# Local attention masks laid into two PSUM banks by ScalarE instead of TensorE, with three of ScalarE's tasks moved in its queue

## The chip, the cores and the metric

The kernel runs on one core of a Trainium2 chip. The metric is the device time of one launch in microseconds (us), the median of several runs. TensorE (PE in the profile) does the matrix products, VectorE (DVE) and ScalarE (ACT) the elementwise work, GpSimd (POOL) more of it, and SyncE's queue (SPq) issues the transfers.

## The reference

The input x is 8 x 256 x 128. After a layer norm xn, the output is x + A(xn) + F(xn). A is one causal attention (16 heads of 64, keys and values through a rank of 128). F is a stack of 6 layers, and nearly all the time goes there. Each layer is

```python
x = attn_layer(shift_tokens(x), Wqkv, q_scale, k_scale, Wo) + x
x = ffn_layer(shift_tokens(x), g, b, W1, b1, W2, b2) + x

# attn_layer: q, k are l2-normalised per head, scaled, rotated; then, in windows of 32 queries
# over 64 keys (the window before and its own):
mask = (it < jb) | (it > jb + w) | (jb == -1)
sim = einsum(q, keys) * 8;  sim = where(mask, -max, sim)
out = einsum(softmax(sim), values)
# ffn_layer: layer norm, a, gate = x @ W1 + b1; (a * gelu(gate)) @ W2 + b2
```

## The kernel before

The causal attention A and the input norm fill the first 335 us. After that a stream of 192 slots, `slot(s)` for s = 0 to 191, does the six layers: a slot is one group of 4 heads of one of the 8 batch elements of one layer (6 x 8 x 4 = 192). The order of each engine's work inside a slot is written out by hand, once per engine, and semaphores tie the engines together. Each slot overlaps stages of several groups. In slot s:

- **TensorE** turns the weights of group s-1 (`turn_windows`, L984: 4 transposes), then computes the scores of group s (`windows`: two bf16 products that put the mask into the two banks of `pair_bank`, L965, and 64 small products that add the scores, L974), the keys of group s+4 (L1005 to L1007), a part of the output projection (L926), the norms of group s+3 (L958), the values times weights of group s-1 (`weigh_windows`, L996), one step of the feed-forward part when there is one (gate product L1057, up product L1071, down product L1079), the queries (L1005 to L1007) and values (L1017 to L1019) of group s+4, and sometimes two products of a layer norm (L1093, L1101).
- **VectorE** takes the maximum of the scores and subtracts it (`shift_windows`, L1289, L1291), rotates the keys (L1310, L1311), sums the exponentials and multiplies by the reciprocal (`weigh_down`, L1296, L1298, L1301, which signals `weights_ready`), bounds the norms (L1390), and rotates the queries when their squares are done (again L1310, L1311). The residual of the feed-forward part (L1325) comes first in a slot with s mod 8 = 5.
- **ScalarE**, in this order: `values_out` (L561, values from PSUM to `v_sb`), `spread_out` (L630, two activations), the table load back to exp and ln in a slot after a GELU (L681), the deviations of a layer norm (L636, L639), the exponential of the scores in place in both banks (L686), ln and exp of the norms (L690, L693), squares of the keys (L621), the rotary tables at a layer change (L601 to L609), the squares of a layer norm (L650), its gain (`gained`, L644), `output_out` (L657, into `yt`), the gate copy (L715), GELU with its table load (L661, L663), the squares of the queries (L621), the GELU of the last third (L667).
- **GpSimd** adds the rotated halves (L431), normalises keys and queries (L424) and adds the squares (L451). At a layer change it also splits the next layer's weights (L412, L419).
- **SyncE's queue** moves the normalised keys and queries into `zqk` (L350, 8 transfers a slot) and the values into `v_late` (L356, L357).

The feed-forward part repeats every 8 slots (`mlp_slot(s, first)`: s mod 8 equals first mod 8, 24 times from `first` on). From slot 13 on the gate copies lie in slots with s mod 8 = 5, 6 and 7, the GELU in those with 0 (22 times inside the stream, slots 16 to 184), and the table load back to exp and ln in those with 1. A layer is 32 slots; there are 5 layer changes.

`turn_windows(n)` waits for `weights_ready` of group n and for `output_out` of group n-1 (`lyt_ready`). `windows(n)` waits for the transfers of its keys and queries (`z_in`) and for `weights_ready` of group n-1, since both use `pair_bank`.

Of the kernel before, what the change touches and what calls it, by code (L numbers as in the profile page):

```python
# [12 lines left out]
ACT = mybir.ActivationFunctionType  # L13
# [3 lines left out]
P = 128  # L17
# [4 lines left out]
G, HG = 4, 4  # L22
# [18 lines left out]
KEYS = 2 * WIN  # L41
# [3 lines left out]
GROUPS = UNITS * G  # L45
# [5 lines left out]
def block_of(slot, x):  # L51

    return 4 * (slot // 2) + slot % 2 + 2 * x
# [48 lines left out]
def build(nc, x, w_kv_down, w_kv_up, w_q, w_out, Wqkv, q_scale, k_scale, Wo, ln_g, ln_b, W1, b1, W2, b2, const, out):  # L102
    with ExitStack() as ctx:
        def sb(name, shape, dt=F32):
            return ctx.enter_context(nc.sbuf_tensor(name, shape, dt))

        def sem(name):
            return ctx.enter_context(nc.semaphore(name))
# [8 lines left out]
        ident_b = sb("ident_b", [P, P], BF16)  # L117
        mask_b = {"causal": sb("mask_causal_b", [P, P], BF16), "local": sb("mask_local_b", [P, 4 * KEYS], BF16)}
# [55 lines left out]
        def ln_n(m):  # L174

            return late_ln if m >= G else gate[:, 0:2, 0:T]

        def rinv(m):

            return late_rinv if m >= G else gate[:, 0:2, T:2 * T]  # L180


        pair_bank = ctx.enter_context(nc.psum_tensor("pair_bank", [P, 2, 512], F32))
        bank = [pair_bank[:, 0, :], pair_bank[:, 1, :]] + [ctx.enter_context(nc.psum_tensor(f"bank{i}", [P, 512], F32)) for i in range(2, 8)]
# [10 lines left out]
        names += """spread_zero w_in split_high split_done rot_par_ready q_tabs_ready k_tabs_ready gain_ready gate_bias_ready out_bias_ready  # L195
            x_high_ready x_split lk_done lq_done lv_done k_prod q_prod k_square q_square sums_ready k_summed q_summed
            n_done ln_done rinv_ready bound_ready zn_ready z_in0 z_in1 z_in2 z_in3 lv_ready v_late_in0 v_late_in1 v_late_in2 v_late_in3
            scores_done top_ready shifted raised sum_ready part_ready weights_ready turned spread_ready lpv_done lyt_ready
            wo_in0 wo_in1 wo_in2 wo_in3 lwo_done lres_done xc_done xc_ready xc_squared var_done ln_var rstd_ready xh_raw xh_ready
            w1_gate_in w1_up_in w2_in gate_done gate_ready gelu_done up_done hid_ready mlp_done mlp_res""".split()  # L200
        S = {n: sem(n) for n in names}
# [3 lines left out]
        def after(eng, name, value):  # L205

            if not (isinstance(value, int) and value <= 0):
                eng.wait_ge(S[name], value)
# [38 lines left out]
        def active(s, first, last):  # L247

            return first <= s < last

        def mlp_slot(s, first):

            return s % (2 * G) == first % (2 * G) and first <= s < first + 2 * G * MLPS

        def layer_begun(s, at):

            l, k = divmod(s - at, LAYER)
            return l + 1 if k == 0 and 0 <= l < DEPTH - 1 else 0
# [253 lines left out]
        def _(act):  # L512
# [41 lines left out]
            def values_out(m):  # L554

                og, odd = m % G, m // G % 2
                act.wait_ge(S["lv_done"], m + 1)
                after(act, "lpv_done", m - 2 * G + 1)
                if m < 2 * G:
                    act.wait_ge(S["pv_done"], STEPS - G if m < G else STEPS)  # L560
                act.activation(v_sb[:, odd, :, og * GW:(og + 1) * GW], B_N[:, :].rearrange("p (t n) -> p t n", t=TT), ACT.Copy).then_inc(S["lv_ready"], 1)  # L561
# [51 lines left out]
            def rotary_tables(l, idx):  # L613

                for part in range(2):
                    rotary_part(l, idx, part)
# [29 lines left out]
            def xc_squares(w):  # L646
# [2 lines left out]
                after(act, "var_done", w)  # L649
                act.activation(xc2[:, :], xc[:, :], ACT.Square).then_inc(S["xc_squared"], 1)  # L650

            def output_out(n):

                og = n % G
                act.wait_ge(S["lpv_done"], n + 1)
                after(act, "lwo_done", n + 1 - G)
                act.activation(yt[:, 2 * og:2 * og + 2, :], B_T.rearrange("p (c t) -> p c t", c=2), ACT.Copy).then_inc(S["lyt_ready"], 1)  # L657

            def gelus(p):

                act.preload_act_table(ACT.Gelu)  # L661
                act.wait_ge(S["gate_ready"], 3 * p + 3)
                act.activation(gate[:, 0:2, :], gate[:, 0:2, :], ACT.Gelu).then_inc(S["gelu_done"], 1)  # L663
# [5 lines left out]
            def slot(s):  # L669
                g = s % G  # L670
                one, two = active(s, -4, GROUPS - 4), active(s, -3, GROUPS - 3)
                three, four = active(s, 0, GROUPS), active(s, 1, GROUPS + 1)
                normed = g == 0 and active(s, 2 * G, 2 * G + GROUPS)
                if two and s >= 0:
                    values_out(s + 3)
                if s == 1:
                    act.wait_ge(S["spread_zero"], 2)
                if four:
                    spread_out(s - 1)
                if mlp_slot(s, 17):  # L680
                    act.preload_act_table_set(LN_EXP)  # L681
                if normed:
                    deviations((s - 8) // G, B_M)
                if three:
                    act.wait_ge(S["shifted"], s + 1)
                    act.activation(both, both, ACT.Exp).then_inc(S["raised"], 1)  # L686
                if two:
                    m = s + 3
                    act.wait_ge(S["n_done"], m + 1)
                    act.activation(ln_n(m), B_N[:, :].rearrange("p (a t) -> p a t", a=2), ACT.Ln, bias=tiny[:, 0:1], scale=LNS).then_inc(S["ln_done"], 1)  # L690
                    act.wait_ge(S["ln_done"], m + 1)
                    after(act, "zn_ready", m)
                    act.activation(rinv(m), ln_n(m), ACT.Exp, scale=-0.5).then_inc(S["rinv_ready"], 1)  # L693
                if one:
                    squares(s + 4, "k_prod", B_K, 1, "k_square")
                l = layer_begun(s, LAYER - 5)
                if l:
                    rotary_scales(l)
                    rotary_tables(l, 1)
                l = layer_begun(s, LAYER - 4)  # L700
                if l:
                    act.wait_ge(S["q_prod"], LAYER * l)
                    rotary_tables(l, 0)
                if g == 3 and active(s, 7, 7 + GROUPS):
                    xc_squares((s - 7) // G)
                if normed:
                    gained((s - 8) // G)
                if four:
                    output_out(s - 1)
                for c in range(3):  # L710
                    if mlp_slot(s, 13 + c):
                        p = (s - 13 - c) // (2 * G)
                        act.wait_ge(S["gate_done"], 3 * p + c + 1)
                        after(act, "hid_ready", 3 * p + c - 2)
                        act.activation(gate[0:CW[c], c, :], B_M[0:CW[c], :], ACT.Identity, bias=gate_bias[0:CW[c], c:c + 1]).then_inc(S["gate_ready"], 1)  # L715
                session = mlp_slot(s, 16)
                if session:
                    gelus((s - 16) // (2 * G))
                if one:
                    squares(s + 4, "lq_done", B_Q, 0, "q_square")  # L720
                if session:
                    last_gelus((s - 16) // (2 * G))
                l = layer_begun(s, LAYER + 6)
                if l:
                    gains(l)
                l = layer_begun(s, LAYER + 10)
                if l:
                    gate_biases(l)
# [64 lines left out]
        def _(pe):  # L793
# [166 lines left out]
            def windows(n, unit, g):  # L960

                pe.wait_ge(S[f"z_in{g}"], 16 * 2 * HG * (unit + 1))
                after(pe, "weights_ready", n)
                for a in range(2):
                    pe.matmul(bank[a][:, 0:4 * KEYS], ident_b[:, :], mask_b["local"][:, :], start=True, stop=True)  # L965
                for pair in range(2):
                    for x in range(2):
                        for tile in range(TILES):
                            j = block_of(tile, x)
                            k0, skip = max(WIN * (j - 1), 0), WIN if j == 0 else 0  # L970
                            at = (2 * pair + x) * KEYS
                            for a in range(2):
                                rows = slice(D * a, D * a + D)
                                mm = pe.matmul(bank[a][WIN * tile:WIN * tile + WIN, at + skip:at + KEYS], zqk[rows, g, 0, pair, WIN * j:WIN * j + WIN],  # L974
                                               zqk[rows, g, 1, pair, k0:WIN * (j + 1)], start=False, stop=True,
                                               tile_position=(D * a, WIN * tile), skip_group_check=True)
                mm.then_inc(S["scores_done"], 1)
# [525 lines left out]
```

## Time and profile before

| | us |
|---|---|
| median of 3 runs | 1941.88 (1940.21 to 1942.47) |
| the profiled execution's own time | 1940.49 |
| its span in the profile | 1938.7 |
| TensorE busy | 1851.4, 95% of the span |
| VectorE busy | 1577.9, 81% |
| ScalarE busy | 1408.8, 73% |
| GpSimd busy | 1368.8, 71% |
| granted TensorE clock, mean | 0.999 |

Matmuls are pipelined, so the busy time of one overlaps the next; what one of them adds to TensorE's queue is the distance from its start to that of the next. The profile's chain that ended last is made of such distances.

### The profile page before, as it was taken

Reading aid. Unit: us, or ns where it says so; the run is one execution under the profiler, and the core shown is the slowest. Engines: PE = TensorE matmul, PEld = TensorE weight load, DVE = VectorE, ACT = ScalarE, POOL = GpSimd, SP = SyncE. Lnnn points to the kernel's source line nnn. Section 1 sums busy time; section 2 is a strip of 40 time slices with the busy share of each in tenths; the row PEclk is TensorE's granted clock in tenths of the full one; section 3 lists DMA queues with packets and bytes.
Section 4 is the critical chain, followed back from the end, with each engine's and each line's share of the span. In section 5 each row is a group of like instructions: output and inputs, shape, how many; then the busy total and the mean of one; then the engine's idle time right before and its main releaser. Section 6 shows DMA issues by size and latency. Waiting matters only on the chain.

```text
span 1938.7 us, 68797 instructions
## 1 busy us (share of the span) xinstructions
PE 1851.4 (95%) x27097; PEld 1394.4 (72%) x27097; DVE 1577.9 (81%) x3052; ACT 1408.8 (73%) x2853; POOL 1368.8 (71%) x1455
## 2 busy tenths in 40 slices
PE   6999998999999999999999999999999999999997
PEld 4777765777767777777777677777677776777774
DVE  5776777888888888788888888888888888888875
ACT  5766665677777777877777777778777777777784
POOL 3010025898798787888787987878887879888770
PEclk9999999999999999999999999999999999999999
DMA  4000001444434334334344343443333443433332
GB/s 131 2 1 0 0 0 39 105 105 103 127 85 110 94 101 128 93 93 104 96 104 123 87 107 97 103 126 94 93 103 96 108 120 88 107 96 102 94 98 67
DMA packets 193542, 171.07 MB, mean 88 GB/s; under 512 B 32304, under 2 KB 190168, under 8 KB 193240
## 3 DMA queue, kind: packets, MB, share of 16 engines
q1 hardware_dynamic: 193240, 166.89, 32.9%
q8 instruction: 209, 3.42, 0.8%
q14 instruction: 93, 0.76, 0.1%
HBM read 21.01 MB, written 1.05 MB: 11 GB/s over the span
## 4 chain that ended last, share of the span: by engine, by line
PE 71%; ACT 12%; issue 7%; DVE 4%; POOL 3%; SPq 3%; DMA 0%; ACTq 0%; POOLq 0%; DVEq 0%
PE bank L996 7%; PE bank L958 7%; PE bank L926 6%; PE pair_bank L974 6%; PE bank L1005 5%; PE bank L984 3%; PE bank L1057 3%; PE bank L1006 3%; PE bank L1007 3%; PE bank L1079 3%; ACT sq L621 2%; SPq L350 2%; PE bank L843 2%; PE bank L1071 2%; ACT probs L690 2%
## 5 line engine op out<-in xcount | busy, mean ns | idle before, releaser
L431 POOL TENSOR_TENSOR z_raw<-rot_u,rot_v 128x256 f32<-128x256 f32 x768 | 553.1, 744 | 100.9 <-DVE rot_v L1311 95.6
L424 POOL TENSOR_TENSOR z_norm<-probs_t,z_raw 128x512 f32<-128x512 f32 x376 | 481.8, 1282 | 92.1 <-DVE probs_t L1390 89.1
L1310 DVE TENSOR_TENSOR rot_u<-bank,tabs 128x512 f32<-128x512 f32 x384 | 263.1, 685 | 165.0 <-ACT sq L621 164.6
L451 POOL TENSOR_TENSOR sqs<-sq 128x512 f32<-128x512 f32 x192 | 246.1, 1282 | 90.0 <-issue 89.4
L1005 PE MATMUL bank<-x_high,w_high 128*128 128x256 f32 x768 | 301.2, 392 | 0.2 <-issue 0.2
L686 ACT ACTIVATE pair_bank<-pair_bank 128x512 f32<-128x512 f32 x192 | 111.7, 582 | 220.4 <-DVE pair_bank L1291 220.1
L1311 DVE TENSOR_TENSOR rot_v<-bank,tabs 128x512 f32<-128x512 f32 x384 | 261.4, 681 | 0.0
L621 ACT ACTIVATE sq<-bank 128x512 f32<-128x512 f32 x384 | 225.2, 588 | 49.8 <-PE bank L1007 43.6
L996 PEld LDWEIGHTS bank<-probs_t,v_late 128*64 128x64 f32 x3072 | 155.0, 137 | 144.4 <-issue 144.4
L630 ACT ACTIVATE probs_t<-bank 64x512 f32<-64x512 f32 x384 | 226.7, 590 | 35.7 <-PE bank L984 33.4
L958 PE MATMUL bank<-sqs,consts 128*128 128x512 f32 x384 | 198.8, 599 | 25.0 <-POOL sqs L451 25.0
L1006 PE MATMUL bank<-x_high,w_low 128*128 128x256 f32 x768 | 216.0, 281 | 0.0
L1007 PE MATMUL bank<-x_low,w_high 128*128 128x256 f32 x768 | 216.0, 281 | 0.0
L996 PE MATMUL bank<-probs_t,v_late 128*64 128x64 f32 x3072 | 198.8, 228 | 0.5 <-ACT probs_t L630 0.5
L926 PE MATMUL bank<-yt,wo 128*128 128x256 f32 x768 | 197.6, 380 | 0.0
L996 PE MATMUL bank<-probs_t,v_sb 128*64 128x64 f32 x3072 | 189.5, 222 | 0.0
L1005 PEld LDWEIGHTS bank<-x_high,w_high 128*128 128x128 f32 x768 | 144.6, 188 | 58.4 <-issue 38.9
L690 ACT ACTIVATE probs<-bank,tiny 128x512 f32<-128x512 f32 x188 | 129.2, 687 | 64.7 <-PE bank L958 62.1
L1289 DVE TENSOR_REDUCE nm<-pair_bank 128x8 f32<-128x512 f32 x192 | 132.1, 688 | 49.3 <-PE pair_bank L974 48.1
L1006 PEld LDWEIGHTS bank<-x_high,w_low 128*128 128x128 f32 x768 | 145.2, 189 | 36.9 <-issue 36.9
L974 PE MATMUL pair_bank<-zqk 64*32 64x64 f32 (+1 forms) x12288 | 163.9, 221 | 0.0
L974 PEld LDWEIGHTS pair_bank<-zqk 64*32 64x32 f32 x12288 | 132.7, 105 | 40.6 <-issue 40.4
(183 smaller groups left out, 4543.4 us busy)
## 6 DMA issues: line engine op xcount, KB each, us to landing
zqk<-z_norm SPq DMA_DIRECT2D x1536, 64.0 KB, 2.1
v_late<-v_sb SPq DMA_DIRECT2D x192, 192.0 KB, 2.6
w_qkv<-in_L_ffn_Wqkv SPq DMA_DIRECT2D x18, 512.0 KB, 4.9
v_late<-v_sb SPq DMA_DIRECT2D x192, 32.0 KB, 2.8
wo<-in_L_ffn_Wo SPq DMA_DIRECT2D x24, 128.0 KB, 2.3
w<-in_L_ffn_W SPq DMA_DIRECT2D x12, 170.5 KB, 2.6
z_norm<-in_L_attn_x SPq DMA_DIRECT2D x4, 256.0 KB, 5.5
w_qkv<-in_L_attn_w_kv_up SPq DMA_DIRECT2D x4, 256.0 KB, 5.0
```

The costliest lines, as they stand in the source:

```text
L424: return pool.tensor_tensor(z_norm[:, parity, idx, :, :], rinv(m)[:, idx, :].unsqueeze(1).broadcast_to([P, 2, T]), z_raw[:, parity, idx, : ...
L431: a = pool.tensor_tensor(z_raw[:, parity, idx, half, :], rot_u[:, idx, half, :], rot_v[:, idx, 1 - half, :], ALU.add)
L621: act.activation(sq[:, idx, :, :], src[:, :].rearrange("p (a t) -> p a t", a=2), ACT.Square).then_inc(S[mark], 1)
L926: mm = pe.matmul(B_X[:, 0:T], wo[:, c, :], yt[:, c, :], start=(c == 0), stop=(c == HD // P - 1))
L958: pe.matmul(B_N[:, :], con("blk"), sqs[:, :, :].rearrange("p a t -> p (a t)"), start=True, stop=True).then_inc(S["n_done"], 1)
L974: mm = pe.matmul(bank[a][WIN * tile:WIN * tile + WIN, at + skip:at + KEYS], zqk[rows, g, 0, pair, WIN * j:WIN * j + WIN], zqk[rows, g, 1, ...
L996: mm = pe.matmul(y[:, t, tile % 2, :, :], (v_sb if tile % 2 else v_late)[:, odd, t, f], spread[:, h, tile, :], start=True, stop=True, tile ...
L1005: pe.matmul(dst, w_high[:, j, cols], x_high[:, odd, :], start=True, stop=False)
L1006: pe.matmul(dst, w_low[:, j, cols], x_high[:, odd, :], start=False, stop=False)
L1007: mm = pe.matmul(dst, w_high[:, j, cols], x_low[:, odd, :], start=False, stop=True)
L1310: dve.tensor_tensor(rot_u[:, idx, :, :], src, tabs[:, 2 * idx, :, :], ALU.mult)
L1311: dve.tensor_tensor(rot_v[:, idx, :, :], src, tabs[:, 2 * idx + 1, :, :], ALU.mult).then_inc(S[mark], 1)
```

## The change

For every slot n with n > 0 and n mod 8 other than 1 (167 of the 192) the mask is no longer put into the banks by the two bf16 products of L965. ScalarE copies it from SBUF (`lay_masks(n)`: one activation, 128 x 512, bf16 to fp32 in `pair_bank`). It does so in slot n-1, behind the gate copies and ahead of the squares of the queries, and waits for `weights_ready` of group n-1. `windows(n)` then waits for a new semaphore, `mask_laid`. In the slots with n mod 8 = 1 TensorE still lays the mask.

In ScalarE's queue, `output_out` moves ahead of the squares of the keys; in the GELU slot the squares of the queries move ahead of the GELU, and so does `values_out` of the next slot; `gained` moves from each slot with s mod 8 = 0 to the slot behind it (in those with s mod 8 = 4 it stays).

```diff
+        def lays_mask(n):
+            return n > 0 and n % (2 * G) != 1
+        def masks_laid(n):
+            return n - (n + 2 * G - 1) // (2 * G)
...
+            def lay_masks(n):
+                act.wait_ge(S["weights_ready"], n)
+                act.activation(pair_bank[:, :, 0:4 * KEYS], mask_b["local"][:, :].unsqueeze(1).broadcast_to([P, 2, 4 * KEYS]), ACT.Copy).then_inc(S["mask_laid"], 1)
...
-                if two and s >= 0:
+                if two and s >= 0 and not mlp_slot(s, 17):
                     values_out(s + 3)
...
+                if four:
+                    output_out(s - 1)
                 if one:
                     squares(s + 4, "k_prod", B_K, 1, "k_square")
...
-                if normed:
+                if normed and s % (2 * G) == G:
                     gained((s - 8) // G)
-                if four:
-                    output_out(s - 1)
+                if s % (2 * G) == 1 and active(s, 9, 9 + GROUPS):
+                    gained((s - 9) // G)
...
-                session = mlp_slot(s, 16)
-                if session:
-                    gelus((s - 16) // (2 * G))
+                if active(s, 0, GROUPS - 1) and lays_mask(s + 1):
+                    lay_masks(s + 1)
                 if one:
                     squares(s + 4, "lq_done", B_Q, 0, "q_square")
-                if session:
+                if mlp_slot(s, 16):
+                    if active(s + 1, -3, GROUPS - 3):
+                        values_out(s + 4)
+                    gelus((s - 16) // (2 * G))
                     last_gelus((s - 16) // (2 * G))
...
             def windows(n, unit, g):
                 pe.wait_ge(S[f"z_in{g}"], 16 * 2 * HG * (unit + 1))
-                after(pe, "weights_ready", n)
-                for a in range(2):
-                    pe.matmul(bank[a][:, 0:4 * KEYS], ident_b[:, :], mask_b["local"][:, :], start=True, stop=True)
+                if lays_mask(n):
+                    pe.wait_ge(S["mask_laid"], masks_laid(n))
+                else:
+                    after(pe, "weights_ready", n)
+                    for a in range(2):
+                        pe.matmul(bank[a][:, 0:4 * KEYS], ident_b[:, :], mask_b["local"][:, :], start=True, stop=True)
```

## Rows read from the trace of the kernel before

**Rows 1.** Busy time of each engine, and the chain that ended last (the page).
```profile
...
PE 1851.4 (95%) x27097; PEld 1394.4 (72%) x27097; DVE 1577.9 (81%) x3052; ACT 1408.8 (73%) x2853; POOL 1368.8 (71%) x1455
...
PE 71%; ACT 12%; issue 7%; DVE 4%; POOL 3%; SPq 3%; DMA 0%; ACTq 0%; POOLq 0%; DVEq 0%
...
```

**Rows 2.** Chain that ended last, one mask: start us, us, what.
```profile
...
1012.63 0.22 PE pair_bank L965 x2
...
```

**Rows 3.** Waits, whole span: us in total, times, longest us.
```profile
...
PE bank L984 <- ACT yt L657: 13.5, 48, 0.7
...
```

**Rows 4.** ScalarE's activations of 512 elements, 800 to 1000 us.
```profile
...
L693 ACT ACTIVATE probs_t<-probs 128x512 f32<-128x512 f32 x24 | 15.1, 631 | 0.8
...
L657 ACT ACTIVATE yt<-bank 128x512 f32<-128x512 f32 x24 | 14.1, 588 | 0.0
L686 ACT ACTIVATE pair_bank<-pair_bank 128x512 f32<-128x512 f32 x24 | 14.0, 582 | 27.3 <-DVE pair_bank L1291 27.2
...
```

**Rows 5.** ScalarE's timeline in slots 84 to 86.
```profile
...
1028.96 0.60 ACT L621 ACTIVATE sq<-bank 128x512 f32<-128x512 f32 x1 [1.76 <-PE bank L1007]
...
1033.80 0.58 ACT L686 ACTIVATE pair_bank<-pair_bank 128x512 f32<-128x512 f32 x1 [2.44 <-DVE pair_bank L1291]
...
1036.62 0.69 ACT L715 ACTIVATE gate<-bank,gate_bias 128x512 f32<-128x512 f32 x1
1037.19 0.61 ACT L621 ACTIVATE sq<-bank 128x512 f32<-128x512 f32 x1
...
1043.56 0.69 ACT L715 ACTIVATE gate<-bank,gate_bias 128x512 f32<-128x512 f32 x1
...
```

**Rows 6.** VectorE's timeline in slot 85.
```profile
...
1029.60 0.69 DVE L1310 TENSOR_TENSOR rot_u<-bank,tabs 128x512 f32<-128x512 f32 x1 [1.26 <-ACT sq L621]
...
1030.80 1.51 DVE L1325 SCALAR_TENSOR_TENSOR xs<-bank,out_bias,xs 64x512 f32<-64x512 f32 x2
...
```

**Rows 7.** TensorE's timeline, first window products of slots 86 and 87.
```profile
...
1037.85 0.84 PE L974 MATMUL pair_bank<-zqk 64*32 64x32 f32 x64
...
1045.89 0.84 PE L974 MATMUL pair_bank<-zqk 64*32 64x32 f32 x64
...
```

**Rows 8.** ScalarE's timeline in slots 88 and 89.
```profile
...
1057.50 0.69 ACT L690 ACTIVATE probs<-bank,tiny 128x512 f32<-128x512 f32 x1 [0.58 <-PE bank L958]
...
1058.75 0.58 ACT L621 ACTIVATE sq<-bank 128x512 f32<-128x512 f32 x1
1059.23 0.59 ACT L644 ACTIVATE xh<-xc,gain 128x256 f32<-128x256 f32 x1
1059.72 0.58 ACT L657 ACTIVATE yt<-bank 128x512 f32<-128x512 f32 x1
1060.32 1.28 ACT L661 ACT_TABLE_LOAD   x1
...
1066.55 0.58 ACT L686 ACTIVATE pair_bank<-pair_bank 128x512 f32<-128x512 f32 x1
...
1069.37 0.60 ACT L621 ACTIVATE sq<-bank 128x512 f32<-128x512 f32 x1
...
```

**Rows 9.** TensorE's timeline at the ends of slots 88 and 89.
```profile
...
1059.89 0.28 PE L1019 MATMUL bank<-w_high,x_low 128*128 128x256 f32 x1
1060.45 0.63 PE L984 MATMUL bank<-consts,probs 128*128 128x128 f32 x4 [0.28 <-ACT yt L657]
...
1070.40 0.81 PE L974 MATMUL pair_bank<-zqk 64*32 64x32 f32 x62
...
```

**Rows 10.** Busy time of each engine in a period with weight splits, and without.
```profile
...
1053.70:1123.00 69.30, 65.31 (x1036) 48.64 (x1034) 58.70 (x98) 52.93 (x97) 63.74 (x65) 1.00 0.35 88
1123.00:1188.70 65.70, 64.28 (x1037) 48.84 (x1036) 55.28 (x99) 49.88 (x88) 52.72 (x57) 1.00 0.40 104
...
```

**Rows 11.** Chain that ended last, slot 30.
```profile
...
577.09 1.10 PE bank L958 x2
...
```

**Rows 12.** Chain that ended last, before slot 10's windows.
```profile
...
406.04 3.71 DMA zqk<-z_norm
...
```

More of the change, by code:

```diff
@@ L197, in build @@
             n_done ln_done rinv_ready bound_ready zn_ready z_in0 z_in1 z_in2 z_in3 lv_ready v_late_in0 v_late_in1 v_late_in2 v_late_in3
-            scores_done top_ready shifted raised sum_ready part_ready weights_ready turned spread_ready lpv_done lyt_ready
+            scores_done mask_laid top_ready shifted raised sum_ready part_ready weights_ready turned spread_ready lpv_done lyt_ready
             wo_in0 wo_in1 wo_in2 wo_in3 lwo_done lres_done xc_done xc_ready xc_squared var_done ln_var rstd_ready xh_raw xh_ready
```

## The prediction

> **What bounds the kernel now.** I read the page first. TensorE is busy for 95% of the span, and the chain that ended last lies on it for 71%, on ScalarE for 12%, on every other engine for little [rows 1]. So I followed that chain in order of time through one period of 8 slots (82 to 89, 1004 to 1070 us). It runs on TensorE without a break from slot 82 into slot 88; there each slot's mask is a piece of 0.22 us between the turn of the weights and the scores [rows 2]. From the norms of slot 88 to the turn behind slot 89 it is on ScalarE: two table loads, the GELUs and everything queued with them [rows 8]. So a product taken from TensorE is worth its 0.22 us only where TensorE is what comes last; I need the places where it isn't.
>
> Three of them show. First, the GELU pair just named. Second, slot 85 (s mod 8 = 5): ScalarE waits 2.44 us for VectorE there and then works through its queue without idle time up to the gate copy [rows 5], because VectorE has the squares of the queries, the rotation and 1.51 us of feed-forward residual ahead of the maximum [rows 6]. Third, layer changes: GpSimd is busy for 63.7 of 69.3 us in such a period and 52.7 of 65.7 in another [rows 10]. And until slot 10 the chain runs through SyncE's transfers, not TensorE [rows 12].
>
> **The ceiling.** 167 masks leave TensorE, 167 x 0.22 = 36.7 us [rows 2]. The granted clock is 1.00 before [rows 10], so nothing is to be had from it.
>
> **The price of the copy.** No activation here goes from SBUF to PSUM. The nearest, all 512 elements wide: PSUM to PSUM 0.58 us, PSUM to SBUF 0.59, SBUF to SBUF 0.63 [rows 4]; with a bias taken from SBUF 0.69 (the gate copy in rows 5). Start to start they take 0.48 us in a full queue [rows 8]. I take 0.59 for the copy and 0.48 for what it holds up; 0.58 and 0.69 are the ends among equal sizes. As a far end, if each element of SBUF to PSUM cost double, I take twice the PSUM copy, 1.18.
>
> The rows show 0.582 into PSUM against 0.588 into SBUF [rows 4]. The Trainium skill (ScalarE: Activation LUTs, Step-by-step: what each stage is for) says that ScalarE reaches PSUM with lower latency than SBUF; by that the copy would be at the cheap end, 0.58, and the sum below 0.4 us better. The same page (What ACT_TABLE_LOAD costs) gives 186 ns + 0.833 ns an element for an activation without pointer operands, an estimate of 0.61 us here; the sum would be 0.7 us worse. Neither decides.
>
> **An ordinary slot.** In slots 82 to 84, 86 and 87 the copy lies behind `weights_ready` and ahead of the squares of the queries, for which ScalarE mostly waits anyway. In slot 86 the gate copy starts at 1043.56 [rows 5], so the mask is in by about 1044.9 even with the 0.23 us by which this queue gets later after slot 85 and 0.14 us for the semaphore; TensorE wants it at 1045.89 - 0.22 [rows 7]. Margin 0.8 us. Where there is no gate copy the mask stands in the old place of `output_out`, which the turn had to wait for before; so it comes in time there too, even behind the rotary tables. Gain: 0.22 us in each of slots 83, 84, 87 and 88, 0.88 less rounding, 0.86 a period.
>
> The copy delays the squares of the queries by up to 0.48, and VectorE's rotation with them. I checked the ring that this could close: rotation 1.2, maximum 0.7, subtraction 0.7, exponentials under the key rotation 1.2, sum and reciprocal 0.95, product 0.7, mask 0.5, squares 0.65, together about 6.6 us (durations of this timeline, all near 0.69 a pass as in rows 6). Slots take 8.2 us on the mean (65.7 / 8 [rows 10]). It doesn't bind.
>
> **Slot 85.** From the squares of slot 84 (1028.96) to the gate copy (1036.62) nothing depends on the masks [rows 5, 6]. The copy takes the place in which the squares of the queries stood, 1037.19, and ends at 1037.78; with 0.14 for the semaphore the scores of slot 86 can start at 1037.92. Before they started at 1037.85 [rows 7]. So the masks of slots 85 and 86, 0.44 us, are lost and 0.07 on top.
>
> **The GELU pair.** Before: `output_out` at 1059.72, table load at 1060.32, exponentials of slot 89 at 1066.55 [rows 8]. After: `output_out` goes to 1058.75, the squares of the keys to 1059.23, those of the queries to 1059.71, and `values_out` waits for the end of the values, 1059.89 + 0.28 [rows 9], so it ends near 1060.80. The load starts at 1060.82, 0.50 later, but two activations (0.96) have left the stretch behind it. The exponentials start at 1066.09, 0.46 earlier. Then ln, exp, copy and squares of slot 89 as before, 2.82 us to where the squares of the queries stood [rows 8], plus 0.49 for `gained` (rows 8 have its distance): mask at 1069.40, done at 1069.99, scores of slot 90 at 1070.13 instead of 1070.40 [rows 9]. Gain 0.27, with slot 90's mask in it. That the turn of slot 89 no longer waits for `yt` (13.5 us in 48 waits [rows 3], 0.28 in this one [rows 9]) pays nothing, since ScalarE's chain comes last. The early squares and values free the norms of slot 89, also under ScalarE's chain.
>
> A period without a layer change: 0.86 + 0.27 - 0.07 = 1.06. There are 16: 17.0 us.
>
> **A layer change.** VectorE's L1390, 0.46 earlier with the exponentials, starts GpSimd on a stretch of work without idle time that ends in the norms of slot 30 (577.09) [rows 11]. What TensorE saves under it is lost. Gain 0.46, and 0.43 for the two masks behind it: 0.9, five times, 4.5 us. In slot 27 (s mod 32 = 27) the layer norm's squares stand 0.48 later, since `output_out` is now ahead of the rotary tables; TensorE waits for them, but again under GpSimd's stretch.
>
> **Start and end.** Up to slot 10 nothing: its transfers land at 409.75 [rows 12]. Slots 10 to 16: 7 masks, 1.5, less some 0.3 in slot 13, a gate slot: 1.2. The last 8 slots: GELU pair 0.27, two masks 0.43, and three more at 0.22 in slots 189 to 191, where the mask is copied under the turn: 1.3.
>
> **The sum.** 1.2 + 17.0 + 4.5 + 1.3 = 24.0 us. Against the profiled execution's 1940.49 that is 1916.5. The median of the runs is 1.4 above it, so the forecast for the median is 1918.
>
> **The rivals.**
> A. *TensorE gets the whole ceiling.* If the queue in slot 85 has more slack than I read (another start of VectorE's chain, a shorter copy), its masks count too: 22 x 0.51 = 11 us more, 1907. For: TensorE alone fills the chain of that slot in the trace. Against: ScalarE has no idle time between 1033.80 and the gate copy. Chance 0.1.
> B. *The copy costs more.* Every 0.1 us over 0.59 comes back in slots 85 and 89, some 37 times outside the layer changes: 3.7 us. With 0.69 the time is 1922, with 0.8 it is 1926, with 1.18 1940. Chance of a result from 1926 to 1938: 0.1.
> C. *Slower.* The same queue, with a copy from 1.24 us on (0.59 + 24.0/37), makes the kernel slower: the ring above reaches 7.3 and ScalarE decides slots 85, 86 and 89. At 1.4 us it is 1948. Nothing of 512 elements in the trace takes more than 0.69, which speaks against it. Chance 0.07.
> D. *Nothing comes of it.* TensorE's freed time turns into idle time ahead of L974 in every slot, because the mask is always the last of its waits; 1942. For: ScalarE waits little in slots 85 and 89. Against: the 0.8 us of margin in slot 86. Chance 0.05.
>
> **How the numbers follow.** My forecast, in its own range of 1912 to 1925, has 0.68. The range of 8 in 10 reaches from rival A to half of B: 1907 to 1930. A measurement of this kernel tells 0.2% (4 us) from no change. Faster: 0.68 + 0.1 + 0.1 = 0.88; within 0.2%: D, 0.05; slower: C, 0.07.
>
> **What would show it.** The copy, 167 times, mean near 0.59. Starts of L974: 7.8 us apart from slot 82 to 84 where they were 8.0, and from 86 to 88; the two slots to 86 together as long as before; the pair to slot 90 0.3 us shorter. In the chain that ended last, ScalarE in slot 85 (gate copy, mask), where there was only TensorE. In waits, TensorE's L974 on the mask copy some 40 times, a few tenths of a us each. I am wrong if L974 waits in slots 87 and 88 too, if the copy takes over 0.7, or if GpSimd's stretch at a layer change gets longer than its 0.46 of a head start.

## The result and the profile after

The changed kernel takes 1924.82 us in the median of 4 runs (1922.0 to 1925.9) beside 1941.16 for the kernel before: a ratio of 0.9913 (95% interval 0.9896 to 0.993). Measured again with 5 runs it is 1923.81, ratio 0.9917 (0.9903 to 0.993). So it is faster by 16 to 17 us; I had forecast 24, and a median of 1918. The 1924.8 lies inside my own range of 1912 to 1925, but only just.

The page of the changed kernel, engines and the chain that ended last, against [rows 1]:

```profile
...
PE 1813.2 (94%) x26763; PEld 1373.4 (72%) x26763; DVE 1572.1 (82%) x3052; ACT 1480.1 (77%) x3020; POOL 1374.0 (72%) x1455
...
PE 59%; ACT 18%; DVE 11%; issue 9%; SPq 1%; POOL 1%; DMA 0%; ACTq 0%; DVEq 0%; POOLq 0%
...
```

TensorE lost 38 us of busy time, and yet its share of the chain fell from 71% to 59%: ScalarE went from 12 to 18% and VectorE from 4 to 11%.

A table made from the traces says where the time went. It holds the distance from the first score product (L974, here L994) of one slot to that of the next, by s mod 8: medians over the 16 ordinary periods between slots 16 and 184, then the mean period, and that of the 5 periods with a layer change.

```
                 0>1   1>2   2>3   3>4   4>5   5>6   6>7   7>8   period   layer change   slots 0 to 16
before           7.23  9.18  8.04  8.01  9.33  7.62  8.05  8.10  65.67    69.32          119.7
after            6.77  9.39  7.95  7.82  9.14  7.93  7.84  7.90  64.77    69.03          119.2
order only       6.78  8.70  8.45  8.01  9.33  7.62  8.05  8.10  65.13    69.08          120.3
masks only       7.25  8.96  7.97  7.80  9.14  7.92  7.84  7.89  64.84    69.04          121.5
TensorE 2, 6     6.78  8.69  8.24  7.81  9.14  7.62  7.83  7.89  64.03    68.52          121.4
no masks         6.55  8.70  8.45  7.80  9.14  7.41  7.83  7.89  63.90    68.50          117.7
TensorE 6        6.78  9.39  7.95  7.85  9.14  7.62  7.83  7.89  64.49    69.06          120.0
gain late        6.77  8.90  8.04  7.79  9.14  7.93  7.84  7.89  64.37    68.59          119.5
spare copy       6.86  9.60  7.95  7.83  9.14  8.23  7.84  8.04  65.50    69.34          120.5
both, gain late  6.77  8.70  8.24  7.80  9.14  7.63  7.83  7.89  64.06    68.40          119.2
```

The copy itself, every instruction of its line (durations in ns, lowest, median, highest), and who waited for it (us, times):

```profile
L663 ACT ACTIVATE pair_bank<-mask_local_b x167: 577/601/616, 352.2 to 1886.2; 128x512 f32<-128x512 bf16 x167
...
  PE pair_bank L994: 29.6, 46
...
```

167 copies of 0.601 us, which is the price I took. TensorE waits for 46 of them, 0.64 us each: in this trace 24 times ahead of the scores of slots with s mod 8 = 2 and 22 times ahead of those with s mod 8 = 6. The timelines show one of each. ScalarE about slot 85, against [rows 5]:

```profile
...
1022.04 0.60 ACT L629 ACTIVATE sq<-bank 128x512 f32<-128x512 f32 x1 [1.28 <-PE bank L1027]
...
1026.88 0.58 ACT L699 ACTIVATE pair_bank<-pair_bank 128x512 f32<-128x512 f32 x1 [2.44 <-DVE pair_bank L1311]
...
1029.69 0.69 ACT L730 ACTIVATE gate<-bank,gate_bias 128x512 f32<-128x512 f32 x1
1030.26 0.61 ACT L663 ACTIVATE pair_bank<-mask_local_b 128x512 f32<-128x512 bf16 x1
1030.78 0.61 ACT L629 ACTIVATE sq<-bank 128x512 f32<-128x512 f32 x1
...
```

VectorE is waited for as before (2.44), the queue is full up to the gate copy, and the mask stands where the squares of the queries stood. The squares come 0.52 later. For the pair of slots 88 and 89, against [rows 8]:

```profile
...
1050.28 0.69 ACT L703 ACTIVATE probs<-bank,tiny 128x512 f32<-128x512 f32 x1 [0.45 <-PE bank L975]
...
1053.61 1.28 ACT L674 ACT_TABLE_LOAD   x1
...
1058.88 0.58 ACT L699 ACTIVATE pair_bank<-pair_bank 128x512 f32<-128x512 f32 x1
...
1061.69 0.60 ACT L652 ACTIVATE xh<-xc,gain 128x256 f32<-128x256 f32 x1
1062.19 0.60 ACT L663 ACTIVATE pair_bank<-mask_local_b 128x512 f32<-128x512 bf16 x1
1062.71 0.59 ACT L629 ACTIVATE sq<-bank 128x512 f32<-128x512 f32 x1
...
```

From the ln of slot 88 to the table load it is 3.33 us where it was 2.82, from that load to the exponentials 5.27 where it was 6.23. The exponentials come 0.45 earlier against the ln (8.60 instead of 9.05), and `gained` and the mask then stand ahead of the squares. TensorE's timeline has the other end of both, the scores of slots 86 and 90, against [rows 7, 9]:

```profile
...
1031.02 0.72 PE L994 MATMUL pair_bank<-zqk 64*32 64x32 f32 x51 [0.46 <-ACT pair_bank L663]
...
1062.93 0.46 PE L994 MATMUL pair_bank<-zqk 64*32 64x32 f32 x35 [0.84 <-ACT pair_bank L663]
...
```

From the squares of slot 84 to these scores it is 8.98 us (before 8.89); from the ln of slot 88 to the scores of slot 90 it is 12.65 (before 12.90).

### The profile page after: what moved, and what is told of

Read it like the earlier page. It is cut to its first block, busy times and chain, and to the rows that moved or that the text cites. A ratio compares the mean times of both kernels' runs of the same rounds, so it can differ in the third digit from the quotient of the medians.

```text
span 1920.2 us, 68296 instructions
## 1 busy us (share of the span) xinstructions
PE 1813.2 (94%) x26763; PEld 1373.4 (72%) x26763; DVE 1572.1 (82%) x3052; ACT 1480.1 (77%) x3020; POOL 1374.0 (72%) x1455
## 3 DMA queue, kind: packets, MB, share of 16 engines
HBM read 21.01 MB, written 1.05 MB: 11 GB/s over the span
## 4 chain that ended last, share of the span: by engine, by line
PE 59%; ACT 18%; DVE 11%; issue 9%; SPq 1%; POOL 1%; DMA 0%; ACTq 0%; DVEq 0%; POOLq 0%
PE bank L975 6%; PE bank L1016 6%; PE bank L943 5%; PE pair_bank L994 5%; PE bank L1025 4%; ACT probs L703 3%; ACT sq L629 3%; PE bank L1027 3%; PE bank L1026 3%; PE bank L1077 2%; PE bank L1099 2%; ACT yt L670 2%; PE bank L1004 2%; PE bank L860 2%; PE bank L1091 2%
## 5 line engine op out<-in xcount | busy, mean ns | idle before, releaser
L432 POOL TENSOR_TENSOR z_norm<-probs_t,z_raw 128x512 f32<-128x512 f32 x376 | 480.8, 1279 | 119.6 <-DVE probs_t L1410 117.4
L459 POOL TENSOR_TENSOR sqs<-sq 128x512 f32<-128x512 f32 x192 | 250.5, 1305 | 71.0 <-issue 70.9
L994 PE MATMUL pair_bank<-zqk 64*32 64x64 f32 (+1 forms) x12288 | 164.9, 221 | 30.2 <-ACT pair_bank L663 29.6
L994 PEld LDWEIGHTS pair_bank<-zqk 64*32 64x32 f32 x12288 | 134.9, 105 | 65.8 <-issue 64.2
L1016 PEld LDWEIGHTS bank<-probs_t,v_sb 128*64 128x64 f32 x3072 | 158.6, 138 | 0.0
```

What stands on the lines that cost most here:

```text
L432: return pool.tensor_tensor(z_norm[:, parity, idx, :, :], rinv(m)[:, idx, :].unsqueeze(1).broadcast_to([P, 2, T]), z_raw[:, parity, idx, : ...
L1016: mm = pe.matmul(y[:, t, tile % 2, :, :], (v_sb if tile % 2 else v_late)[:, odd, t, f], spread[:, h, tile, :], start=True, stop=True, tile ...
```

## The experiments

My theory after the result: the copy is on the path in two slots of eight, those with n mod 8 = 2 and 6, where ScalarE reaches it late, and what is missing beyond that lies behind the squares of the queries that the copy holds up, on VectorE and GpSimd. Rivals: the masks weren't worth 0.22 us on TensorE; the new order gives the gain and the masks nothing; the copy is late everywhere.

**The order alone.** All masks are TensorE's again.

```diff
         def lays_mask(n):
-            return n > 0 and n % (2 * G) != 1
+            return False
```

> All masks by TensorE again, ScalarE's order as after the change. My theory: the copy's place in the queue costs the pair of slots 89 and 90, so without it the scores of slot 90 start about 0.9 us earlier than before the change (the exponentials 0.46 earlier, output_out ahead of the squares 0.48): ordinary period 64.7 us instead of 65.6, time 1921 to 1926. Rival 1, the order is worth nothing by itself and the gain is all from the masks: 1938 to 1942. Rival 2, order and masks add up: 1932 to 1936.

Measured: 1930.2 us (1929.53 to 1933.59), ratio 0.9948 (0.9935 to 0.9962). A miss for every theory. The pair did what mine said, 15.48 us instead of 16.41. But the slot behind it takes 8.45 instead of 8.04, so that of the 0.93 only 0.52 is left at slot 3 (23.93 against 24.45). Why, the run with 2 and 6 on TensorE shows below: VectorE.

**The masks alone.** ScalarE lays the masks in the same slots; the rest of its queue is in the order of before (the diffs of this section are against the changed kernel).

```diff
-                if two and s >= 0 and not mlp_slot(s, 17):
+                if two and s >= 0:
...
-                if four:
-                    output_out(s - 1)
                 if one:
                     squares(s + 4, "k_prod", B_K, 1, "k_square")
...
-                if normed and s % (2 * G) == G:
+                if normed:
                     gained((s - 8) // G)
-                if s % (2 * G) == 1 and active(s, 9, 9 + GROUPS):
-                    gained((s - 9) // G)
+                if four:
+                    output_out(s - 1)
...
                     lay_masks(s + 1)
+                session = mlp_slot(s, 16)
+                if session:
+                    gelus((s - 16) // (2 * G))
                 if one:
                     squares(s + 4, "lq_done", B_Q, 0, "q_square")
-                if mlp_slot(s, 16):
-                    if active(s + 1, -3, GROUPS - 3):
-                        values_out(s + 4)
-                    gelus((s - 16) // (2 * G))
+                if session:
                     last_gelus((s - 16) // (2 * G))
```

> Masks by ScalarE in the same slots, the rest of ScalarE's queue in the order of before. My theory: slots 83, 84, 87 and 88 gain 0.8 us in an ordinary period, slots 85 and 86 nothing, and the pair about 0.3, since gained then stands in slot 88 and not ahead of the mask in slot 89; time 1922 to 1928, so order and masks don't add up. Rival: without the new order the GELU pair is as long as before or longer and half of the gain is gone, 1930 to 1936.

Measured: 1924.99 us (1924.4 to 1927.03), ratio 0.9919 (0.9905 to 0.9932), the same as the whole change. Order and masks don't add up: alone they give 11 and 16 us, together 16 to 17. With `gained` back in slot 88 the mask of slot 90 gains what the GELU pair loses; TensorE then waits for copies only ahead of the scores of slots with s mod 8 = 6, 22 times. Also, in the layer changes slots 3 to 4 take 8.83 instead of 9.27 with `output_out` back behind the rotary tables, and the period is the same (69.04 against 69.03): that delay of the layer norm's squares is hidden, as I had taken it to be.

**TensorE lays the masks of n mod 8 = 2 and 6 as well.**

```diff
-            return n > 0 and n % (2 * G) != 1
+            return n > 0 and n % (2 * G) not in (1, 2, 6)
...
-            return n - (n + 2 * G - 1) // (2 * G)
+            return sum(lays_mask(k) for k in range(1, n + 1))
```

> As after the change, but TensorE also lays the masks of slots with n mod 8 = 2 and 6. My theory (the copy stands on the path in just these two slots): W(6) comes 0.3 earlier and W(2) 0.7 to 0.9 earlier against after the change, ordinary period 63.6 us; time 1898 to 1906. Rival (the masks are late everywhere or the loss is elsewhere, in VectorE and GpSimd behind the delayed squares): 1918 to 1926, or slower than after by up to 9 us (44 masks of 0.22 more on TensorE).

Measured: 1909.93 us (1908.86 to 1913.0), ratio 0.9842 (0.9829 to 0.9856): 14 us faster than the change, with 48 more masks on TensorE (119 copies are left; my 44 was a miscount). The two places gain what I expected, 0.70 and 0.31 us. The total missed my span by 4 us, since slots 2 to 3 give 0.29 back. TensorE's waits for the copy, 29.6 us in the changed kernel, are gone: the trace lists nobody who waited for the 119.

What comes last behind the pair shows in VectorE's timeline of slots 97 and 98 of this kernel:

```profile
...
1125.28 0.69 DVE L1316 TENSOR_REDUCE rsum<-pair_bank 128x8 f32<-128x512 f32 x1 [1.35 <-ACT pair_bank L699]
...
1128.06 0.75 DVE L1373 SCALAR_TENSOR_TENSOR hid<-bank,out_bias,gate 128x512 f32<-128x512 f32 x1
1128.73 0.68 DVE L1330 TENSOR_TENSOR rot_u<-bank,tabs 128x512 f32<-128x512 f32 x1
...
1134.34 0.74 DVE L1373 SCALAR_TENSOR_TENSOR hid<-bank,out_bias,gate 128x512 f32<-128x512 f32 x1
...
```

Behind the start of the sum of the exponentials (1125.28) no row of VectorE up to the end of the second hidden product (1135.08) has idle time ahead of it. In the chain that ended last, ScalarE has the 9.2 us before that, with both table loads, VectorE these 9.8, and TensorE follows on it:

```profile
...
1116.07 0.70 ACT probs L703
...
1125.28 0.70 DVE rsum L1316
...
1134.42 0.67 DVE hid L1373
...
1135.22 0.67 PE bank L1113 x2
...
```

L1113 is the layer norm's product that stands ahead of the turn and the scores of the next slot; it waits for that hidden product (`hid`). Its start tells who comes last there: in every ordinary period of this run it comes 0.15 us behind the end of the hidden product, as it does in most or all of those of every other version here, and 0.30 behind it in the kernel before.

**No mask at all.** From slot 1 on the mask is left out of the scores, so this isn't the reference's computation; it is a bound.

```diff
-            return n > 0 and n % (2 * G) != 1
+            return False
...
                 else:
                     after(pe, "weights_ready", n)
-                    for a in range(2):
-                        pe.matmul(bank[a][:, 0:4 * KEYS], ident_b[:, :], mask_b["local"][:, :], start=True, stop=True)
+                    if n == 0:
+                        for a in range(2):
+                            pe.matmul(bank[a][:, 0:4 * KEYS], ident_b[:, :], mask_b["local"][:, :], start=True, stop=True)
```

> No mask is laid by either engine from slot 1 on (left out of the computation), ScalarE's order as after. The bound of what the masks can give. My theory: ordinary period 63.0 us, 2.6 less than before (six masks at 0.22 and the pair by 1.3), time 1880 to 1890. Rival (TensorE is not what comes last in slots 83 to 88, VectorE's ring is): over 1900, the period not under 64.

Measured: 1904.96 us (1902.96 to 1906.87), ratio 0.9816 (0.9803 to 0.9829). My number missed by 15 us. The rival's time held, but not its reason, and its period (not under 64) only nearly, 63.90. Slots 3 to 8 give 1.04 for their five masks (40.07 against 41.11), 0.21 each: the price per mask is right, and TensorE does come last there. Slots 0 to 3 give 0.75 for three and the shorter pair together, where I had counted 1.5: they can't go below 23.70, with masks on TensorE (23.71) or without.

**TensorE lays those of n mod 8 = 6 only in addition.**

```diff
-            return n > 0 and n % (2 * G) != 1
+            return n > 0 and n % (2 * G) not in (1, 6)
...
-            return n - (n + 2 * G - 1) // (2 * G)
+            return sum(lays_mask(k) for k in range(1, n + 1))
```

> As after the change, but TensorE also lays the mask of slots with n mod 8 = 6. My theory: slots 4 to 6 together 16.76 us again as in the run with both moved, instead of 17.07, nothing else changes; time 1917 to 1920. Rival (the two moved masks only pay together): same as after, 1923 to 1926.

Measured: 1920.18 us (1918.53 to 1922.99), ratio 0.9897 (0.988 to 0.9913). Slots 4 to 6 take 16.76 instead of 17.07, as expected, and nothing else in the period moves by more than 0.03; the time is 0.2 us over my span. Of TensorE's 46 waits for the copy 24 are left, all ahead of slots with s mod 8 = 2 (us in total, times, longest):

```profile
...
PE pair_bank L994 <- ACT pair_bank L663: 19.4, 24, 0.8
...
```

**`gained` behind the squares of the queries** in slots with s mod 8 = 1; the masks as in the change.

```diff
-                if s % (2 * G) == 1 and active(s, 9, 9 + GROUPS):
-                    gained((s - 9) // G)
...
                 if one:
                     squares(s + 4, "lq_done", B_Q, 0, "q_square")
+                if s % (2 * G) == 1 and active(s, 9, 9 + GROUPS):
+                    gained((s - 9) // G)
```

> As after the change, but gained stands behind the squares of the queries in slots with s mod 8 = 1. My theory (mask copy and gained ahead of the squares hold up VectorE and GpSimd): the pair 0.45 shorter, slots 0 to 3 together near 23.75 instead of 24.11, and a layer change gains as well, 0.3 or more; time 1914 to 1919. Rival (VectorE alone sets slots 0 to 3 after the exponentials): nothing, 1923 to 1926.

Measured: 1914.87 us (1913.99 to 1916.77), ratio 0.9863 (0.9846 to 0.9879). As my theory said: slots 0 to 3 take 23.71, the pair 0.49 less, and a layer change 0.44 less. The mask of n mod 8 = 2 is still ScalarE's in this run, and TensorE still waits for it 24 times, 0.33 us each; yet slots 0 to 3 are as short as without any mask. So that copy costs an ordinary period only because `gained` stands ahead of it and of the squares. The last shows in GpSimd's timeline in slot 25, where it begins its stretch without idle time. Before, the sum of squares (L451) follows the normalised keys at once:

```profile
...
536.83 1.27 POOL L424 TENSOR_TENSOR z_norm<-probs_t,z_raw 128x512 f32<-128x512 f32 x1 [0.68 <-DVE probs_t L1390]
538.05 1.28 POOL L451 TENSOR_TENSOR sqs<-sq 128x512 f32<-128x512 f32 x1
...
```

After the change it comes 1.87 us after them instead of 1.22, with 0.60 idle:

```profile
...
534.78 1.27 POOL L432 TENSOR_TENSOR z_norm<-probs_t,z_raw 128x512 f32<-128x512 f32 x1 [1.92 <-DVE probs_t L1410]
536.65 1.29 POOL L459 TENSOR_TENSOR sqs<-sq 128x512 f32<-128x512 f32 x1 [0.60 <-issue]
...
```

With `gained` behind the squares, 1.39:

```profile
...
536.42 1.27 POOL L432 TENSOR_TENSOR z_norm<-probs_t,z_raw 128x512 f32<-128x512 f32 x1 [1.95 <-DVE probs_t L1410]
537.81 1.29 POOL L459 TENSOR_TENSOR sqs<-sq 128x512 f32<-128x512 f32 x1
...
```

**A spare copy.** Ahead of each mask copy ScalarE also copies the mask once into an unused tile. It is 256 elements wide, half of the mask copy, so it costs the queue 0.3 us and not the 0.5 that my expectation names (the lines that set up the tile and its semaphore are left out).

```diff
...
                 act.wait_ge(S["weights_ready"], n)
+                after(act, "spare_done", masks_laid(n) - 1)
+                act.activation(spare[:, :], mask_b["local"][:, :], ACT.Copy).then_inc(S["spare_done"], 1)
```

> As after the change, with one more copy of the same mask, into an unused tile in SBUF, ahead of each of the 167 mask copies: what ScalarE does for a mask takes some 0.5 us longer. My theory: only slots 5 and 1 (mod 8) have no margin, so an ordinary period gets 1.0 to 1.2 longer, time 1943 to 1950. Rival (the copy is on the path in every slot): 3 us a period, over 1980. Rival (ScalarE has room everywhere): under 1930.

Measured: 1938.78 us (1936.64 to 1939.48), ratio 0.9986 (0.9977 to 0.9996); my span is missed, mostly by the wrong size. ScalarE's timeline of this kernel:

```profile
...
1036.06 0.69 ACT L733 ACTIVATE gate<-bank,gate_bias 128x512 f32<-128x512 f32 x1
1036.63 0.42 ACT L665 ACTIVATE spare<-mask_local_b 128x256 f32<-128x256 bf16 x1
1036.94 0.61 ACT L666 ACTIVATE pair_bank<-mask_local_b 128x512 f32<-128x512 bf16 x1
...
```

0.31 from the start of the spare copy to that of the mask. Slots 0 to 2 together get 0.30 longer and slots 5 to 6 0.30, 7 to 8 0.14, the others nothing; a layer change gets 0.31. 16 x 0.73 + 5 x 0.31 = 13.2 of the 14 us. The copy is on the path in two slots, and hardly elsewhere (0.14 of 0.31 in a third). TensorE's waits for it:

```profile
...
PE pair_bank L997 <- ACT pair_bank L666: 45.9, 52, 1.1
...
```

**Both repairs together.** TensorE lays 1, 2 and 6; `gained` stands behind the squares.

> TensorE lays the masks of n mod 8 = 2 and 6 as before in this study, and gained stands behind the squares of the queries in slots with s mod 8 = 1. My theory: slots 0 to 3 are set by the table loads and then by VectorE (23.7 us, as without any mask), so an ordinary period stays at 64.0; the layer changes may gain up to 0.5 each; 1907 to 1911. Rival (the squares of the queries still hold up slots 1 to 3): period 63.7 or less, 1900 to 1905.

Measured: 1908.3 us (1905.19 to 1909.27), ratio 0.9828 (0.9812 to 0.9845), the lowest time of a version that computes the reference, 33 us ahead of the kernel before. The 1.6 us to the version without the move of `gained` are within what the two intervals leave open. The ordinary period stays at 64.06 against 64.03. So in this one the squares hold nothing up; a layer change takes 68.40 instead of 68.52.

**The two kernels once more.**

> The changed kernel itself once more, for its median and to see how far slots 0 to 16 differ between two executions of one kernel. My theory: slots 16 to 184 repeat to 0.5 us; slots 0 to 16, where the transfers into zqk set the pace, differ by 1 us or more, so that no gain or loss under 1.5 us can be read there; median 1923.5 to 1926. Rival: slots 0 to 16 repeat too (119.2), and the 0.9 us that were missing there are the change's.

> The kernel before once more, one profile. My theory: slots 16 to 184 as in the first trace, slots 0 to 16 off by up to 2 us from 119.7, and the low clock in the last 20 us (1.7 us) may be there or not. Rival: all stretches repeat to 0.3 us.

Measured: 1923.81 us for the changed kernel (5 runs), 1940.6 for the one before. Slots 16 to 184: 1381.9 (1381.5 in the first trace) and 1397.7 (1397.3), so they repeat to 0.5 and their difference is 15.8. But slots 0 to 16 repeat as well, 119.0 and 119.2, 119.6 and 119.7. My theory of that stretch fell: by these two pairs of traces the 0.5 us there are a result. Their place isn't: up to slot 10 the changed kernel took 74.3 and 73.5 us, the one before 74.3 and 73.9. What doesn't repeat is a low clock at the end. The windows of the feed-forward products that follow on slot 191 hold, beside busy times, the granted clock; before, it was 0.61 in the mean of 4.4 us:

```profile
...
1920.00:1924.40 4.40, 4.40 (x9) 1.79 (x8) 1.95 (x4) 2.77 (x4) 0.00 (x0) 0.61 0.19 60
...
```

In the changed kernel's first trace it was 1.00, and these products take 2.58 us in the chain instead of 4.27:

```profile
...
1903.30:1907.60 4.30, 4.30 (x15) 2.09 (x14) 3.46 (x7) 3.13 (x5) 0.00 (x0) 1.00 0.19 61
...
```

In its second trace it was back:

```profile
...
1902.90:1907.20 4.30, 4.30 (x9) 1.69 (x8) 1.88 (x4) 2.77 (x4) 0.00 (x0) 0.60 0.20 61
...
```

So 1.7 us of the 18.5 between the two profiled spans (1938.7 and 1920.2) are not the change's, and the median of 16 to 17 is the truer number.

## Why the prediction came out as it did

The direction and the mechanism in the slots that I looked at were right, and the range held by 0.2 us (1.2 in the second measurement), which is luck as much as judgement; the size was 24.0 against 16 to 17. The two terms that carry the difference are both about the squares of the queries, which I let come later at no cost. By its terms:

- **The ceiling, 0.22 us a mask.** Right, where TensorE comes last: 0.21 each in the kernel without masks.
- **The price of the copy, 0.59, and 0.48 for what it holds up.** Measured 0.601 and 0.52. Rivals B and C are out with it. The slope that I gave them, 3.7 us for 0.1, was somewhat low: the spare copy cost 14 us for 0.31, 4.5 for 0.1. By the Trainium skill (ScalarE: Activation LUTs, What ACT_TABLE_LOAD costs) I had an estimate of 0.61, and this trace agrees to 0.01. Its other rule, that PSUM is the nearer port (same page, Step-by-step: what each stage is for), makes no difference that these runs show.
- **The margin in slot 86, 0.8.** By rows 5 an activation starts 0.57 behind a gate copy and not 0.48, so my terms give 1045.1 and 0.6. Measured 0.65 (the copy of slot 86 starts at 1037.46, the scores of slot 87 at 1038.86). Slots 86 and 87 had the room, as forecast.
- **Slot 85.** Forecast 8.96 us from the squares of slot 84 to the scores of slot 86, measured 8.98; in the table slots 4 to 6 are 0.12 longer, where I had 0.07. Rival A, that these two masks count after all, fell with that, and the run with the mask of slot 86 on TensorE confirms it from the other side.
- **The GELU pair.** Forecast 12.63 from the ln of slot 88 to the scores of slot 90, measured 12.65.
- **An ordinary period, 1.06.** Measured 0.90, so 14.4 instead of 17.0. The step that failed: "It doesn't bind", said of the delayed squares. I had looked for a ring that would be longer than a slot, and none was shown. But behind the GELU pair VectorE is not in such a ring: it starts late, behind the exponentials, and L1113 had only 0.15 us of slack to it before (0.30 behind the hidden product, where 0.15 is the least). Its timeline in slot 89 after the change, and the chain that ended last there:

```profile
...
1062.28 0.75 DVE L1373 SCALAR_TENSOR_TENSOR hid<-bank,out_bias,gate 128x512 f32<-128x512 f32 x1
1063.33 0.69 DVE L1330 TENSOR_TENSOR rot_u<-bank,tabs 128x512 f32<-128x512 f32 x1 [0.30 <-ACT sq L629]
...
```

```profile
...
1061.69 0.60 ACT xh L652
1062.29 0.49 ACT pair_bank L663
1062.79 0.53 ACT sq L629
...
1063.33 0.69 DVE rot_u L1330
...
```

The rotation of the queries waits 0.30 for squares that stand behind `gained` and the mask. It starts 1.05 behind the start of the hidden product, 0.67 in the run with 2 and 6 on TensorE. The wait is there in all 16 ordinary periods and all 5 layer changes of the changed kernel, in none of the kernel before, the order alone, the masks alone or `gained` late, and is 0.61 with the spare copy. (Slot 89 opens a period with a layer change.) In the ordinary periods L1113, now 0.15 behind the hidden product, starts 0.04 later after the scores of slot 2 (mod 8) than before, and the turn 0.51 behind L1113 instead of 0.42, as in every version in which VectorE comes last there; why the turn does isn't shown. Together they are the 0.13 by which slots 2 to 3 gain 0.09 instead of 0.22. Slots 0 to 3 take 24.11. Without the wait they take 23.70, of which ScalarE's table loads and then VectorE's own work are the floor.

- **A layer change, 0.9.** Measured 0.29, 1.5 us instead of 4.5: the largest error, 3 of the 7 us. The term had 0.46 up to the norms of slot 30 and 0.43 behind them. The second was right (0.43). The first had the wrong sign: from the scores of slot 24 to those norms it is 55.50 us before and 55.63 after. I had let GpSimd's stretch start 0.46 earlier with VectorE's L1410 (L1390 before), and the normalisation that opens the stretch did start 0.46 earlier, counted from the scores of slot 24. The second thing that it needs, the squares of the queries for its sum, had moved back by `gained` and the mask. So the last sign of being wrong on my own list came true: the stretch got 0.59 longer, more than its head start of 0.46. The step that failed is the same as above, a delay of the squares put at nothing. The run with `gained` behind the squares gives 0.44 of it back, nearly all of it ahead of those norms (55.21).
- **Start, 1.2.** Measured 0.5. The chain that ended last after the change shows the same three in a row there, copy, squares, rotation:

```profile
...
409.58 0.60 ACT pair_bank L663
410.17 0.52 ACT sq L629
...
410.72 0.69 DVE rot_u L1330
...
```

Whether they cost the missing 0.7 isn't shown. Slots 0 to 16 took from 117.7 (no masks) to 121.5 us (masks only), not in the order of the rest, and no experiment took that stretch apart.

- **End, 1.3.** Measured 0.7 (50.7 against 51.4); the step from slot 189 to 190 took 0.15 more there (5.73 against 5.58), not 0.22 less.
- **Rival D**, that every freed time turns into a wait ahead of the scores, fell: waits of TensorE for the copy are in two slots of eight only.

16 x 0.90 + 5 x 0.29 + 0.5 + 0.7 = 17.1 us, beside 16.3 and 17.2 in the medians. Of the 6.9 missing, the layer changes have 3.0, the ordinary periods 2.6, start and end 1.3.

## What to carry to other kernels

Work moved off the busiest engine pays per place, not per count: of seven moved masks in a period two cost more on ScalarE than they saved on TensorE, and leaving just those where they were gave 14 us, nearly as much as the whole change. One of the two costs an ordinary period nothing once the task ahead of it in the queue is moved away, so the place isn't a property of the mask but of the order around it. Find such places by asking of each place whether the receiving queue has idle time between what releases it and what waits for it. And an operation put ahead of another in a full queue delays everyone who reads the other: follow each reader, also on engines that look loosely filled, in the stretch where it has just been held up, not on its average.

## What the runs showed of the hardware

An activation from SBUF (bf16) to PSUM (fp32), 512 elements over two banks from 256 repeated ones, takes 0.601 us (0.577 to 0.616) and 0.52 from its start to the next; one of 256 elements from SBUF to SBUF 0.42 and 0.31. The granted TensorE clock had a mean of 0.60 to 0.61 over some 4.3 us behind slot 191 in three of four traces of the two kernels, since it was at the lower of its two levels (1.2 GHz) for most of that (0.50 from 1920.3 to 1923.5 us in the first trace of the kernel before), after single products for which TensorE had waited on VectorE and ScalarE; in one trace, with the same waits ahead, it stayed at 1.00.
